# Layer-0 attentions: the keys are spread over the heads by ScalarE from the accumulator

## The chip, the cores and the metric

The kernel runs on one core of one Trainium2 chip, in fp32 throughout. The metric is the device time of one execution in microseconds. Before the change the median of three runs is 1980.87 us (1977.02 to 1982.0).

## The reference, cut to what matters

A two-layer perceiver block over 64 sequences of 32 queries with 256 features, 16 heads of 16 features, and a context of 257 rows. Each layer is a cross-attention, a self-attention and an FFN, each with a layernorm ahead and a residual. What the change touches are the two attentions of layer 0:

```python
# cross-attention X0: causal mask over the first 32 context rows
q = (layernorm(x) @ Wq.T + bq); k = (ctx @ Wk.T + bk); v = (ctx @ Wv.T + bv)     # 16 heads of 16
sm = softmax(where(causal, -inf, q k^T / sqrt(16)))
x = x + (sm v) @ Wo.T + bo
# self-attention A0: as above, with a bias by distance and a sigmoid gate
q, k, v = split(layernorm(x) @ Wqkv + bqkv)
out = softmax(q k^T / 4 + pos_bias, causal) v
x = x + (out * sigmoid(layernorm(x) @ Wgate + bgate)) @ Wout + bout
```

## The kernel before, in words

The 64 sequences of 32 rows lie in 16 tiles of 128 rows (4 sequences each, `SPT`). Both attentions of layer 0 run over the 16 tiles as 4 rounds of 4 lanes (`run_lanes`, `SLOTS0` = 20 slots). A tile's work is cut into steps with a slot each; lane `l` runs 5 slots behind lane `l-1`. Every engine walks the same slots and issues its steps in that fixed order; the engines meet through semaphores. Per stretch of five slots each engine handles one tile's worth of work, made up of steps of four different lanes.

Per tile, in the order of slots: VectorE takes statistics (slot 0) and normalizes (1, `d_scale`); TensorE turns the tile (2, `p_turn`, L408) and ScalarE copies it (3, L787); TensorE projects queries, keys and values, and in A0 the gate (4, `p_project`, L396), into the lane's two PSUM banks, transposed: features on partitions, rows on columns. ScalarE then evacuates (5, `a_keys`, `a_values`, `a_gate`): two instructions for the keys into `kT` (L796, with bias), two for the queries (L799, scale 0.25 and bias), two for the values (L807), in A0 two more for the gate (L825). VectorE (6, `d_keys`, L1020) multiplies `kT` into `kbd`: every key block of 32 columns is written four times, each copy multiplied with one of the four columns of `mask_hr`, which keeps the features of one head in each half of the partitions; so one matmul on `kbd` gives the scores of four heads. Behind it VectorE transposes the values (6, L1026), which GpSimd spreads (7, L1444). TensorE makes the scores (8, `p_scores`, L474) when `k_masked`, `qT_copied` and `v_copied` are there. VectorE adds the mask (9, L1052), takes the negative maximum (L1061) and subtracts (L1065); ScalarE takes the exponential (10, L831); VectorE sums (11, L1070); TensorE turns the probabilities (11, L483), ScalarE copies them (12, L835), TensorE multiplies with the values (13, L493), VectorE normalizes (14, L1089), TensorE turns (15, L502), ScalarE copies in X0 (16, L813) or VectorE multiplies with the gate in A0 (16, L1097), TensorE projects out (17, `p_out`, L402), VectorE adds to x (18, L1102).

So, where several lanes meet, ScalarE's order in one stretch of five slots is: exponential of one lane, then keys, queries, values (and gate) of another, then the copy L813 of a third (X0), the copy L835 of the first, the copy L787. VectorE's order is: statistics, in A0 L1097, sums, `d_keys`, value transpose, normalization, in A0 the gate's reciprocal (L1083) and addition (L1078), in A0 between them pieces of the quantization of FFN weights, L1102, L1089, mask, maximum, subtraction. TensorE's is: turn of the output, turn of the probabilities, output projection, turn, values, scores, projection.

Of the kernel before, what the change touches and what calls it, by code (L numbers as in the profile page):

```python
# [11 lines left out]
ALU = mybir.AluOpType  # L12
ACT = mybir.ActivationFunctionType
AX = mybir.AxisListType

P = 128
D = 256
KI = D // P
NSEQ = 64
L = 32  # L20
S = 257
T = NSEQ * L // P
SPT = P // L
H = 16
HD = D // H
G = 4
J = H // G
# [16 lines left out]
def perceiver(nc, A, out):  # L44
    ctx = ExitStack()
    with ctx:
        def sb(name, shape, dt=F32):
            return ctx.enter_context(nc.sbuf_tensor(name, shape, dt))

        def sem(name):  # L50
            return ctx.enter_context(nc.semaphore(name))
# [8 lines left out]
        mask_hr = sb("mask_hr", [P, 4])  # L60
        mask4 = sb("mask4", [P, 4])
# [7 lines left out]
        colb = sb("colb", [P, 10, KI])  # L69
        BQ0, BK0, BV0, BQA, BKA, BVA, BG, BQ1, BK1, BV1 = range(10)  # L70
        a1_bv = sb("a1_bv", [P, KI])
        nbg = sb("nbg", [P, KI])
        qb = sb("qb", [P, 2, KI])
        rowb = sb("rowb", [P, 4, D])
        BO0, BOA, BO1, BOB = range(4)
        a1_bqk = sb("a1_bqk", [P, 2 * D])
# [14 lines left out]
        def view(at, *shape):  # L91
            size = 1
            for s in shape:
                size *= s
            assert at + size <= RSIZE
            v = R[:, at:at + size]
            if len(shape) == 2:
                v = v.rearrange("p (a b) -> p a b", b=shape[1])
            elif len(shape) == 3:
                v = v.rearrange("p (a b c) -> p a b c", b=shape[1], c=shape[2])  # L100
            elif len(shape) == 4:
                v = v.rearrange("p (a b c d) -> p a b c d", b=shape[1], c=shape[2], d=shape[3])
            return v

        def put(at, sizes):
            places = []
            for s in sizes:
                places.append(at)
                at += s
            return places  # L110


        lane_at = [put(l * LANE, [256, 256, 2048, 512, 1024, 512, 256, 256, 256, 512]) for l in range(NL)]
# [4 lines left out]
        vq = [view(a[1], D) for a in lane_at]  # L118
        kbd = [view(a[2], 2048) for a in lane_at]
        om = [view(a[2], D) for a in lane_at]  # L120
        kT = [view(a[3], D) for a in lane_at]
        qT1 = [view(a[3], 512) for a in lane_at]
        pT = [view(a[3], G, P) for a in lane_at]
        vbd = [view(a[4], H, J * HD) for a in lane_at]
# [24 lines left out]
        a = put(W0, [512] * 4 + [1536, 512, 512])  # L149
# [29 lines left out]
        a = put(0, [256, 256, 512] + [KI * S] * 6 + [512] * 4 + [G * S] * 2 + [1024, 64, 256, 128, 128])  # L179
# [16 lines left out]
        a = put(R1, [KI * F1, KI * F1, NF1 * F1])  # L196
        f_w1, f_w2 = view(a[0], KI, F1), view(a[1], KI, F1)
        f_h1 = view(a[2], NF1, F1)
        a = put(0, [1024, 1024, 4096, 4096, 1024, 512, NF1 * F1, NF1 * D])
# [21 lines left out]
        posmask_ready, gate_bias_ready, pl_scale_ready, consts_made = map(  # L221
            sem, ("posmask_ready", "gate_bias_ready", "pl_scale_ready", "consts_made"))
# [3 lines left out]
                 "probs_ready sum_ready pT_ready pT_copied o_ready o_normed oT_ready oT_copied oT_gated "  # L226
                 "gate_exp gate_plus gate_done y_ready x_updated "
                 "lines_in lines_mul lines_step lines_sq lines_sum q_slots k_slots "
                 "qk_slots_ready q_evac kT_copied").split()
        s = {n: sem(n) for n in names}  # L230


        def tile(n, l):

            return NL * n + l + 1
# [52 lines left out]
        X0, A0, A1 = "x0", "a0", "a1"  # L288
# [3 lines left out]
        def run_lanes(eng, slots, stages):  # L292


            lag = slots // NL

            def a_round(i, steps, i_behind, steps_behind):
                for slot in range(slots):
                    for l in sorted(range(NL), key=lambda l: -((slot - lag * l) % slots)):

                        of_round, n = (steps_behind, i_behind) if slot < lag * l else (steps, i)
                        for at, step in of_round:
                            if at == (slot - lag * l) % slots:
                                step(l, n)

            behind = ()
            for enter, steps in stages:
                enter()
                a_round(0, steps, NT - 1, behind)
                with eng.Fori(1, NT) as i:  # L310
                    a_round(i, steps, i - 1, steps)
                behind = steps
            a_round(NT, (), NT - 1, behind)

        BASE = {X0: 0, A0: NT, A1: 2 * NT}
# [5 lines left out]
        BIAS_K = {X0: BK0, A0: BKA}  # L321
# [3 lines left out]
        bank = [[ps[:, 2 * l + i, :] for i in range(2)] for l in range(NL)]  # L325
# [454 lines left out]
        def _(act):  # L780
            for m in free["act"]:
                act.sem_inc(m, 1)
            af = nc.scalar.activation
# [5 lines left out]
            def a_keys(kind, l, n):  # L789
                if kind == A1:  # L790
                    act.wait_ge(s["qk_slots_ready"], tile(n - BASE[A1], l))
                    af(qT1[l], bank[l][0], ACT.Copy).then_inc(s["qT_copied"], 1)
                    return
                act.wait_ge(s["qk_ready"], tile(n, l))
                for fo in range(KI):
                    af(kT[l][:, fo * P:(fo + 1) * P], bank[l][0][:, (KI + fo) * P:(KI + fo + 1) * P],  # L796
                       ACT.Identity, bias=colb[:, BIAS_K[kind], fo:fo + 1]).then_inc(s["kT_copied"], 1)
                for fo in range(KI):
                    r = af(qT[l][:, fo * P:(fo + 1) * P], bank[l][0][:, fo * P:(fo + 1) * P],  # L799
                           ACT.Identity, scale=0.25, bias=qb[:, BIAS_Q[kind] // BQA, fo:fo + 1])  # L800
                r.then_inc(s["qT_copied"], 1)
# [33 lines left out]
                af(pT[l], bank[l][1].rearrange("p (g t) -> p g t", t=P), ACT.Copy).then_inc(s["pT_copied"], 1)  # L835

            act.wait_ge(in_const, 16 * N_CONST)
            act.wait_ge(gate_bias_ready, 3)
            act.wait_ge(consts_made, 1)

            def attention(kind, steps):
# [9 lines left out]
            for m in range(3):  # L851
                for c in range(3):
                    act.wait_ge(wT_turned, 3 * m + c + 1)
                    at = WT + 1536 * m + 512 * c
                    af(view(at, 512), ps[:, (3 * m + c) % 8, :], ACT.Copy).then_inc(wT_copied, 1)
            ugb = ug.rearrange("p f (b t) -> p f b t", t=BLK)
            with act.Fori(0, NB // 2) as i:
                for u in range(2):
                    b = 2 * i + u
# [10 lines left out]
            for f in range(NF0):  # L870
                af(ug[:, f + NF0, :], ug[:, f + NF0, :], ACT.Identity, scale=qinv[:, QG:QG + 1],
                   bias=magic[:, :]).then_inc(f0_gr, 1)
# [15 lines left out]
            with act.Fori(0, NF0) as f:  # L888
                af(ug[:, f + NF0, :], ug[:, f + NF0, :], ACT.Identity, scale=qinv[:, QS:QS + 1],
                   bias=magic[:, :]).then_inc(f0_g2r, 1)  # L890
            act.wait_ge(f0_scale, 4)
            with act.Fori(0, NB // 2) as i:
                for u in range(2):
                    b = 2 * i + u
# [3 lines left out]
                    for f in range(NF0):  # L898
                        af(oq[u][:, f, :], ugb[:, f, b, :], ACT.Identity, scale=qinv[:, QO:QO + 1],
                           bias=magic[:, :]).then_inc(f0_or, 1)  # L900
# [4 lines left out]
            for fo in range(KI):  # L905
                r = af(c_vlast[:, fo, :], ps[:, 2, fo * NSEQ:(fo + 1) * NSEQ], ACT.Identity,
                       bias=colb[:, BV1, fo:fo + 1])
# [80 lines left out]
        def _(dve):  # L988
            for m in free["dve"]:
                dve.sem_inc(m, 1)  # L990
            v = nc.vector
# [15 lines left out]

            def d_keys(kind, l, i, n):

                if kind == A1:  # L1010
                    dve.wait_ge(s["qk_slots_ready"], tile(n - BASE[A1], l))
                    k = bank[l][1].rearrange("p (c k) -> p c k", k=L).unsqueeze(2).broadcast_to([P, H, J, L])
                    m = mask4[:, :].unsqueeze(1).unsqueeze(3).broadcast_to([P, H, J, L])
                    v.tensor_tensor(kbd[l].rearrange("p (c j k) -> p c j k", j=J, k=L), k, m, ALU.mult)\
                        .then_inc(s["k_masked"], 1)
                    return
                dve.wait_ge(s["kT_copied"], KI * tile(n, l))
                k = kT[l].rearrange("p (c k) -> p c k", k=L).unsqueeze(2).broadcast_to([P, 8, 4, L])
                m = mask_hr[:, :].unsqueeze(1).unsqueeze(3).broadcast_to([P, 8, 4, L])
                v.tensor_tensor(kbd[l][:, 0:8 * P].rearrange("p (c h k) -> p c h k", h=4, k=L), k, m, ALU.mult)\  # L1020
                    .then_inc(s["k_masked"], 1)

            def d_turn_values(kind, l, i, n):
# [128 lines left out]
            def attention(kind, steps, enter=lambda: None):  # L1152
                return (enter, [(at, lambda l, i, step=step: step(
                    kind, l, i, i + (NORM if step in (d_norm, d_scale) else BASE)[kind])) for at, step in steps])
# [5 lines left out]
            v.tensor_scalar(nbg[:, :], colb[:, BG, :], -1.0, None, ALU.mult).then_inc(gate_bias_ready, 1)  # L1160
            for n, at in enumerate((BQ0, BQA)):
                v.tensor_scalar(qb[:, n, :], colb[:, at, :], 0.25, None, ALU.mult).then_inc(gate_bias_ready, 1)
            dve.wait_ge(in_x, 32)

            def enter_a0():
# [8 lines left out]
                dve.wait_ge(in_w["nat"], 48)  # L1174

            run_lanes(dve, SLOTS0, [
                attention(X0, [(0, d_norm), (1, d_scale), (6, d_keys), (6, d_turn_values), (9, d_mask), (9, d_max),
                               (9, d_shift), (11, d_sums), (14, d_norm_out), (18, d_add)]),
                attention(A0, [(0, d_norm), (1, d_scale), (6, d_keys), (6, d_turn_values), (7, d_gate1), (9, d_mask),
                               (9, d_max), (9, d_shift), (11, d_sums), (12, d_gate2), (14, d_norm_out),  # L1180
                               (16, d_gate_out), (18, d_add),
                               (2, d_w_max), (3, d_w_scale), (4, d_w_inverse), (8, d_w_divide), (12, d_w_round),
# [20 lines left out]
            for t in range(T):  # L1203
                r = v.tensor_scalar(xall[:, t, :], x[:, t, :], f_mv[:, t, 0:1], f_rstd[:, t:t + 1],
                                    ALU.subtract, ALU.mult)
# [5 lines left out]
            with dve.Fori(0, NB // 2) as i:  # L1211
                for u in range(2):
                    b = 2 * i + u
# [41 lines left out]
            with dve.Fori(0, NB // 2) as i:  # L1255
                for u in range(2):
                    b = 2 * i + u
# [10 lines left out]
            for par2 in range(2):  # L1268
                r = v.tensor_copy(c_kT[par2][:, :, S - 1], colb[:, BK1, :])
# [91 lines left out]
            for l in range(NL):  # L1361
                v.memset(qs[l], 0.0)
                r = v.memset(ks[l], 0.0)
# [277 lines left out]
```

## Time and profile before

| | |
|---|---|
| median of three runs | 1980.87 us |
| the profiled execution | 1977.1 us |
| its span | 1975.1 us |
| TensorE busy | 1587.7 us (80%) |
| VectorE busy | 871.9 us (44%) |
| ScalarE busy | 568.4 us (29%) |
| GpSimd busy | 522.9 us (26%) |
| mean granted clock of TensorE | 0.906 |
| X0 | about 21 to 140 us |
| A0 | about 140 to 305 us |

The profile is that of one execution. Shares of the whole span say little here, since the stages have different limits: the layer-1 cross-attention and FFN make up most of the span. What matters for X0 and A0 is read within their stretches: busy time by stretch, the instructions in order of time, and the chain of waits that ended last. An engine name in brackets at the end of a timeline row is what released the instruction after the idle time given.

### The profile page before, as it was taken

The page shows a single profiled execution, that of the slowest core. Times are in us where ns is not written, and L with a number is a line of the kernel's source. Part 1 is how long each engine was busy: PE and PEld are TensorE (multiplying, and loading weights), DVE is VectorE, ACT ScalarE, POOL GpSimd, SP SyncE. Part 2 cuts the span into 40 slices and gives each one's busy share as a digit, 9 for nine tenths or more (in the row PEclk, how much of TensorE's full clock was granted, in tenths as well). Part 3 has the DMA queues.
Part 4 walks back from the last instruction along what each step waited for, and adds up shares of the span by engine and source line. Part 5 has one row for each costly group of instructions (what it writes and reads, how often), then busy time and mean ns, then how long its engine had stood idle before and what let it go on. Part 6 is the DMA issues. An engine that isn't in the chain of part 4 may idle for free.

```text
span 1975.1 us, 31007 instructions
## 1 busy us (share of the span) xinstructions
PE 1587.7 (80%) x11788; PEld 1013.7 (51%) x11788; DVE 871.9 (44%) x1668; ACT 568.4 (29%) x1401; POOL 522.9 (26%) x587
## 2 busy tenths in 40 slices
PE   4887775890078999999994566667999999999999
PEld 3676653340067677777772444443445445445445
DVE  3889997337823565555554555553101101100100
ACT  2443332338323445444441111112111111111100
POOL 2443331006103444444443555551000000000000
PEclk9999997995589999999995777778999999999999
DMA  6000000000004111111100000002000000000000
GB/s 234 20 6 2 1 0 1 0 0 0 0 0 178 40 41 37 37 38 42 37 22 1 1 1 0 0 0 107 0 0 11 0 0 11 0 0 11 0 0 11
DMA packets 17765, 43.96 MB, mean 22 GB/s; under 512 B 2992, under 2 KB 5552, under 8 KB 16944
## 3 DMA queue, kind: packets, MB, share of 16 engines
q1 hardware_dynamic: 17712, 43.24, 6.6%
q8 instruction: 35, 0.57, 0.1%
q14 instruction: 18, 0.15, 0.0%
HBM read 41.14 MB, written 2.10 MB: 22 GB/s over the span
## 4 chain that ended last, share of the span: by engine, by line
PE 63%; DVE 16%; issue 9%; POOL 6%; ACT 4%; DVEq 1%; DMA 1%; SPq 0%; POOLq 0%; ACTq 0%
PE ps L754 22%; PE ps L396 12%; PE ps L603 6%; PE ps L609 6%; PE ps L629 4%; PE ps L402 3%; PE ps L769 3%; PE ps L573 3%; POOL lrn L1534 2%; PE ps L640 2%; DVE R L1005 2%; DVE R L1083 1%; POOL R L1524 1%; DVE nmx L1061 1%; DVE R L1233 1%
## 5 line engine op out<-in xcount | busy, mean ns | idle before, releaser
L754 PE MATMUL ps<-R 128*128 128x512 f32 x1024 | 440.6, 592 | 0.0
L396 PE MATMUL ps<-R 128*128 128x128 f32 (+1 forms) x1344 | 317.0, 396 | 7.7 <-ACT R L864 3.3
L754 PEld LDWEIGHTS ps<-R 128*128 128x128 f32 x1024 | 194.3, 190 | 243.5 <-issue 243.5
L396 PEld LDWEIGHTS ps<-R 128*128 128x128 f32 x1344 | 195.3, 199 | 126.7 <-issue 122.5
L1400 DVE TENSOR_TENSOR R<-ps,w3s 128x256 f32<-128x256 f32 x16 | 6.8, 425 | 465.1 <-PE ps L769 465.1
L1494 POOL TENSOR_TENSOR R<-R,c_inv 128x1024 f32<-128x1024 f32 x64 | 122.3, 1911 | 228.6 <-DVE c_inv L1338 228.6
L1303 DVE COPY R<-ps 128x512 f32<-128x512 f32 x128 | 88.5, 692 | 127.7 <-PE ps L629 127.7
L927 ACT ACTIVATE R<-ps,c_nmx 128x257 f32<-128x257 f32 x256 | 118.0, 474 | 89.7 <-DVE c_nmx L1327 89.7
L573 PE MATMUL ps<-R 128*128 128x256 f32 x192 | 50.0, 428 | 109.7 <-DVE R L1196 109.7
L609 PE MATMUL ps<-x_wv,R 128*128 128x256 f32 x512 | 131.2, 380 | 0.0
L603 PE MATMUL ps<-R,x_wk 128*128 128x256 f32 x512 | 125.2, 387 | 3.9 <-POOL R L1486 1.6
L1444 POOL TENSOR_TENSOR R<-R,mask 128x1024 f32<-128x1024 f32 x48 | 93.2, 1941 | 61.6 <-DVE R L1026 61.6
L603 PEld LDWEIGHTS ps<-R,x_wk 128*128 128x128 f32 x512 | 94.2, 192 | 23.1 <-issue 9.2
L573 PEld LDWEIGHTS ps<-R 128*128 128x128 f32 x192 | 41.6, 219 | 118.5 <-issue 104.9
L1555 POOL TENSOR_SCALAR g_ve<-g_mv 128x4 f32<-128x4 f32 x4 | 0.9, 231 | 355.7 <-DVE g_mv L1382 355.7
L609 PEld LDWEIGHTS ps<-x_wv,R 128*128 128x128 f32 x512 | 87.8, 191 | 7.0
L629 PE MATMUL ps<-ident,R 128*128 128x128 f32 x512 | 82.3, 284 | 5.0 <-DVE R L1303 2.6
L1486 POOL TENSOR_TENSOR R<-R 128x512 f32<-128x512 f32 x64 | 66.5, 1039 | 73.2 <-DMA R<-in_ctxT 73.2
L1327 DVE TENSOR_REDUCE c_nmx<-ps 128x2 f32<-128x514 f32 x128 | 82.3, 684 | 4.1 <-PE ps L619 4.0
L408 PE MATMUL ps<-ident,R 128*128 128x128 f32 x96 | 25.2, 353 | 70.2 <-DVE R L1005 70.2
L979 ACT ACTIVATE R<-ps,ffn_s 128x512 f32<-128x512 f32 x32 | 22.0, 687 | 197.5 <-PE ps L754 197.5
L831 ACT ACTIVATE R<-R 128x512 f32<-128x512 f32 x48 | 30.2, 630 | 168.7 <-DVE R L1065 168.7
(174 smaller groups left out, 2373.8 us busy)
## 6 DMA issues: line engine op xcount, KB each, us to landing
R<-in_ctxT SPq DMA_DIRECT2D x64, 257.0 KB, 2.7
R<-in_f_h SPq DMA_DIRECT2D x2, 4096.0 KB, 15.6
R<-in_f_w SPq DMA_DIRECT2D x3, 1024.0 KB, 8.4
R<-in_ctxk SPq DMA_DIRECT2D x16, 128.0 KB, 2.2
out<-x SPq DMA_DIRECT2D x4, 512.0 KB, 2.6
x<-in_x SPq DMA_DIRECT2D x1, 1792.0 KB, 9.2
R<-in_a_wqkv SPq DMA_DIRECT2D x1, 768.0 KB, 8.7
R<-in_w_up SPq DMA_DIRECT2D x1, 768.0 KB, 9.7
```

What stands on the lines that cost most here:

```text
L396: r = mm(dst, w[:, ki, fo * P:(fo + 1) * P], src[:, ki, :], start=(ki == 0), stop=(ki == KI - 1))
L573: r = mm(ps[:, 4 * u + t, 0:D], oq[u][:, f, t * P:(t + 1) * P], wdT[:, f, :], start=(f == 0), stop=(f == NF0 - 1))
L603: r = mm(ps[:, 4, fo * D:(fo + 1) * D], x1_wk[:, ki, fo * P:(fo + 1) * P], c_ctx[u][:, ki, 0:2 * P], start=(ki == 0), stop=(ki == KI - 1))
L609: r = mm(ps[:, 5, c * D:(c + 1) * D], c_ctx[u][:, ki, c * P:(c + 1) * P], x1_wv[:, ki, :], start=(ki == 0), stop=(ki == KI - 1))
L629: r = tr(ps[:, 6, at:at + P], c_p[par][:, g, c * P:(c + 1) * P], ident[:])
L754: r = mm(ps[:, ring[o % 4], :], w[:, k, o * P:(o + 1) * P], src[:, k, :], start=(k == 0), stop=(k == NF1 - 1))
L927: af(c_p[par][:, g, :], ps[:, g, 0:S], ACT.Exp, bias=c_nmx[par][:, g:g + 1], accum_out=c_sum[par][:, g:g + 1]).then_inc(c_exp, 1)
L1303: v.tensor_copy(c_pT[:, 2 * k:2 * k + 2, :, :].rearrange("p g c t -> p (g c t)"), ps[:, 6, :])\
L1327: v.tensor_reduce(c_nmx[u % 2][:, 2 * half:2 * half + 2], ps[:, 2 * half:2 * half + 2, 0:S], AX.X, ALU.max, negate=True).then_inc(c_max, 1)
L1444: p.tensor_tensor(vbd[l].rearrange("p c (r e) -> p c r e", e=HD), vq[l].rearrange("p (c e) -> p c e", e=HD).unsqueeze(2).broadcast_to([P, ...
L1486: p.tensor_tensor(c_ctx[u][:, :, 0:S - 1], c_ctx[u][:, :, 0:S - 1], c_ctx[u][:, :, S - 1:S].broadcast_to([P, KI, S - 1]), ALU.subtract).th ...
L1494: p.tensor_tensor(c_p[u % 2][:, :, 0:S - 1], c_p[u % 2][:, :, 0:S - 1], c_inv[u % 2][:, :].unsqueeze(2).broadcast_to([P, G, S - 1]), ALU.m ...
```

## The change

`a_keys` of X0 and A0 no longer writes `kT`. For each of the two halves of the features, ScalarE reads the projected keys in PSUM four times, once for each head column `h`, and writes them to their places in `kbd` (blocks of 32 columns, 128 apart) with the per-partition scale `mask_hr[:, h]` and a per-partition bias `kb`, which is the key bias times the same mask. The last of the eight instructions signals `k_masked`. VectorE's `d_keys` stays for the attention of layer 1 only; the buffer `kT` and its semaphore go. `kb` is made by two small VectorE operations at the start, and ScalarE waits for five instead of three signals of that kind before it begins. Queries, values and all else keep their code and order.

```diff
--- before.py
+++ after.py
@@ -71,6 +71,7 @@
         a1_bv = sb("a1_bv", [P, KI])
         nbg = sb("nbg", [P, KI])
         qb = sb("qb", [P, 2, KI])
+        kb = sb("kb", [P, 2, KI, 4])
         rowb = sb("rowb", [P, 4, D])
         BO0, BOA, BO1, BOB = range(4)
         a1_bqk = sb("a1_bqk", [P, 2 * D])
@@ -118,7 +119,6 @@
         vq = [view(a[1], D) for a in lane_at]
         kbd = [view(a[2], 2048) for a in lane_at]
         om = [view(a[2], D) for a in lane_at]
-        kT = [view(a[3], D) for a in lane_at]
         qT1 = [view(a[3], 512) for a in lane_at]
         pT = [view(a[3], G, P) for a in lane_at]
         vbd = [view(a[4], H, J * HD) for a in lane_at]
@@ -226,7 +226,7 @@
                  "probs_ready sum_ready pT_ready pT_copied o_ready o_normed oT_ready oT_copied oT_gated "
                  "gate_exp gate_plus gate_done y_ready x_updated "
                  "lines_in lines_mul lines_step lines_sq lines_sum q_slots k_slots "
-                 "qk_slots_ready q_evac kT_copied").split()
+                 "qk_slots_ready q_evac").split()
         s = {n: sem(n) for n in names}
 
 
@@ -793,8 +793,12 @@
                     return
                 act.wait_ge(s["qk_ready"], tile(n, l))
                 for fo in range(KI):
-                    af(kT[l][:, fo * P:(fo + 1) * P], bank[l][0][:, (KI + fo) * P:(KI + fo + 1) * P],
-                       ACT.Identity, bias=colb[:, BIAS_K[kind], fo:fo + 1]).then_inc(s["kT_copied"], 1)
+                    k = bank[l][0][:, (KI + fo) * P:(KI + fo + 1) * P].rearrange("p (b k) -> p b k", k=L)
+                    spread = kbd[l][:, fo * SPT * P:(fo + 1) * SPT * P].rearrange("p (b h k) -> p h b k", h=4, k=L)
+                    for h in range(4):
+                        r = af(spread[:, h], k, ACT.Identity, scale=mask_hr[:, h:h + 1],
+                               bias=kb[:, BIAS_K[kind] // BQA, fo, h:h + 1])
+                r.then_inc(s["k_masked"], 1)
                 for fo in range(KI):
                     r = af(qT[l][:, fo * P:(fo + 1) * P], bank[l][0][:, fo * P:(fo + 1) * P],
                            ACT.Identity, scale=0.25, bias=qb[:, BIAS_Q[kind] // BQA, fo:fo + 1])
@@ -835,7 +839,7 @@
                 af(pT[l], bank[l][1].rearrange("p (g t) -> p g t", t=P), ACT.Copy).then_inc(s["pT_copied"], 1)
 
             act.wait_ge(in_const, 16 * N_CONST)
-            act.wait_ge(gate_bias_ready, 3)
+            act.wait_ge(gate_bias_ready, 5)
             act.wait_ge(consts_made, 1)
 
             def attention(kind, steps):
@@ -1007,17 +1011,10 @@
 
             def d_keys(kind, l, i, n):
 
-                if kind == A1:
-                    dve.wait_ge(s["qk_slots_ready"], tile(n - BASE[A1], l))
-                    k = bank[l][1].rearrange("p (c k) -> p c k", k=L).unsqueeze(2).broadcast_to([P, H, J, L])
-                    m = mask4[:, :].unsqueeze(1).unsqueeze(3).broadcast_to([P, H, J, L])
-                    v.tensor_tensor(kbd[l].rearrange("p (c j k) -> p c j k", j=J, k=L), k, m, ALU.mult)\
-                        .then_inc(s["k_masked"], 1)
-                    return
-                dve.wait_ge(s["kT_copied"], KI * tile(n, l))
-                k = kT[l].rearrange("p (c k) -> p c k", k=L).unsqueeze(2).broadcast_to([P, 8, 4, L])
-                m = mask_hr[:, :].unsqueeze(1).unsqueeze(3).broadcast_to([P, 8, 4, L])
-                v.tensor_tensor(kbd[l][:, 0:8 * P].rearrange("p (c h k) -> p c h k", h=4, k=L), k, m, ALU.mult)\
+                dve.wait_ge(s["qk_slots_ready"], tile(n - BASE[A1], l))
+                k = bank[l][1].rearrange("p (c k) -> p c k", k=L).unsqueeze(2).broadcast_to([P, H, J, L])
+                m = mask4[:, :].unsqueeze(1).unsqueeze(3).broadcast_to([P, H, J, L])
+                v.tensor_tensor(kbd[l].rearrange("p (c j k) -> p c j k", j=J, k=L), k, m, ALU.mult)\
                     .then_inc(s["k_masked"], 1)
 
             def d_turn_values(kind, l, i, n):
@@ -1160,6 +1157,9 @@
             v.tensor_scalar(nbg[:, :], colb[:, BG, :], -1.0, None, ALU.mult).then_inc(gate_bias_ready, 1)
             for n, at in enumerate((BQ0, BQA)):
                 v.tensor_scalar(qb[:, n, :], colb[:, at, :], 0.25, None, ALU.mult).then_inc(gate_bias_ready, 1)
+            for n, at in enumerate((BK0, BKA)):
+                v.tensor_tensor(kb[:, n, :, :], colb[:, at, :].unsqueeze(2).broadcast_to([P, KI, 4]),
+                                mask_hr[:, :].unsqueeze(1).broadcast_to([P, KI, 4]), ALU.mult).then_inc(gate_bias_ready, 1)
             dve.wait_ge(in_x, 32)
 
             def enter_a0():
@@ -1174,9 +1174,9 @@
                 dve.wait_ge(in_w["nat"], 48)
 
             run_lanes(dve, SLOTS0, [
-                attention(X0, [(0, d_norm), (1, d_scale), (6, d_keys), (6, d_turn_values), (9, d_mask), (9, d_max),
+                attention(X0, [(0, d_norm), (1, d_scale), (6, d_turn_values), (9, d_mask), (9, d_max),
                                (9, d_shift), (11, d_sums), (14, d_norm_out), (18, d_add)]),
-                attention(A0, [(0, d_norm), (1, d_scale), (6, d_keys), (6, d_turn_values), (7, d_gate1), (9, d_mask),
+                attention(A0, [(0, d_norm), (1, d_scale), (6, d_turn_values), (7, d_gate1), (9, d_mask),
                                (9, d_max), (9, d_shift), (11, d_sums), (12, d_gate2), (14, d_norm_out),
                                (16, d_gate_out), (18, d_add),
                                (2, d_w_max), (3, d_w_scale), (4, d_w_inverse), (8, d_w_divide), (12, d_w_round),
```

## Rows read from the trace of the kernel before

**Rows 1.** Stretches in X0, A0: us, busy us by engine (instructions), clock, DMA share, GB/s
```profile
21.00:137.00 116.00, 95.02 (x1473) 79.06 (x1474) 89.88 (x176) 50.00 (x148) 52.40 (x61) 1.00 0.16 57
149.00:305.00 156.00, 115.65 (x1625) 94.92 (x1624) 150.51 (x302) 54.69 (x171) 52.66 (x59) 0.96 0.00 1
```

**Rows 2.** Chain of waits within X0, 90 to 106 us: start, us, what
```profile
92.37 0.70 DVE R L1065
93.10 0.63 ACT R L831
...
94.63 0.64 ACT R L807 x2
...
97.54 0.68 PE ps L474 x32
...
99.69 0.70 DVE R L1065
```

**Rows 3.** Timeline of X0, same tile: start, us, engine, line, operation, [idle before <-releaser]
```profile
94.65 1.16 DVE L1020 TENSOR_TENSOR R<-R,mask_hr 128x1024 f32<-128x1024 f32 x1
...
95.60 1.13 PE L402 MATMUL ps<-R 128*128 128x256 f32 x4 [1.16 <-ACT R L813]
95.73 0.43 DVE L1026 STREAM_TRANSPOSE R<-R 128x256 f32<-128x256 f32 x1
```

**Rows 4.** Timeline of A0, ninth of its sixteen tiles and the last
```profile
227.44 0.69 DVE L1065 TENSOR_TENSOR R<-R,nmx 128x512 f32<-128x512 f32 x1
...
228.16 0.63 ACT L831 ACTIVATE R<-R 128x512 f32<-128x512 f32 x1 [5.57 <-DVE R L1065]
...
229.69 0.64 ACT L807 ACTIVATE R<-ps,colb 128x128 f32<-128x128 f32 x2
...
230.49 1.16 DVE L1020 TENSOR_TENSOR R<-R,mask_hr 128x1024 f32<-128x1024 f32 x1
...
231.57 0.43 DVE L1026 STREAM_TRANSPOSE R<-R 128x256 f32<-128x256 f32 x1
...
301.47 0.69 DVE L1065 TENSOR_TENSOR R<-R,nmx 128x512 f32<-128x512 f32 x1
...
304.84 0.43 DVE L1026 STREAM_TRANSPOSE R<-R 128x256 f32<-128x256 f32 x1
```

**Rows 5.** ScalarE: single instructions, then groups by form (busy us, mean ns)
```profile
93.63 0.35 ACT L796 ACTIVATE R<-ps,colb 128x128 f32<-128x128 f32 x1
93.88 0.36 ACT L796 ACTIVATE R<-ps,colb 128x128 f32<-128x128 f32 x1
...
L871 ACT ACTIVATE R<-R,magic,qinv 128x2048 f32<-128x2048 f32 x6 | 12.0, 2082 | 2.0 <-DVE qinv L1191 2.0
...
L883 ACT ACTIVATE R<-R,magic 128x2048 f32<-128x2048 f32 x6 | 11.6, 1985 | 0.0
```

**Rows 6.** TensorE in A0, timeline; then stretches: us, busy, clock, DMA share, GB/s
```profile
221.74 0.44 PE L408 MATMUL ps<-ident,R 128*128 128x128 f32 x2 [1.48 <-DVE R L1005]
...
222.69 0.67 PE L474 MATMUL ps<-R 64*32 64x128 f32 x32
...
232.35 0.69 PE L408 MATMUL ps<-ident,R 128*128 128x128 f32 x2 [1.30 <-DVE R L1005]
...
233.98 1.11 PE L474 MATMUL ps<-R 64*32 64x128 f32 x32
...
230.00:240.00 10.00, 8.70 (x104) 0.66 0.00 0
...
1263.00:1264.00 1.00, 0.00 (x0) 1.00 0.00 0
...
1265.00:1266.00 1.00, 0.69 (x2) 0.50 0.00 0
```

**Rows 7.** VectorE at the start, timeline
```profile
18.30 0.43 DVE L998 BATCH_NORM_STATS2 stats<-x 128x6 f32<-128x256 f32 x1 [8.11 <-DMA x<-in_x]
...
28.15 1.23 DVE L1020 TENSOR_TENSOR R<-R,mask_hr 128x1024 f32<-128x1024 f32 x1 [6.45 <-ACT R L796]
```

## The prediction

> **What bounds the kernel now.** The change touches only the two attentions of layer 0, X0 (cross-attention, from about 21 to 140 us) and A0 (self-attention, to about 305 us), sixteen tiles each. I read the busy time by stretch first [rows 1]. VectorE is busy for 89.88 of 116 us in X0 and for 150.51 of 156 us in A0, ScalarE for 50.00 and 54.69. By shares alone one would take VectorE for the bound of both stages and ScalarE for an engine with half its time to give away. In X0 a quarter of VectorE is idle all the same, so I followed the chain of waits there for one tile [rows 2]. It closes on itself: subtraction of the maximum on VectorE (92.37), exponential on ScalarE (93.10), the evacuations of keys, queries and values of another lane (keys from the exponential's start plus 0.53, values at 94.63), the evacuation of the turned output, the output projection on TensorE (95.60 [rows 3]), turn, values and scores (scores from 97.54), then mask, maximum and subtraction again (99.69). From subtraction to subtraction it is 7.32 us, and ScalarE's key evacuations are a link of it. The VectorE multiply that the change removes is not: it begins at 94.65, and the transpose that follows at 95.73, while TensorE waits 1.16 us for ScalarE [rows 3]. So X0 is bound by a ring through three engines, and ScalarE's order of work stands in it.
>
> In A0 VectorE has little idle time, and its own order is the bound: subtraction at 227.44, the multiply at 230.49, the value transpose at 231.57 [rows 4]. ScalarE runs beside it: exponential at 228.16, values at 229.69. From subtraction to transpose it is 4.13 us in this tile, 3.37 us in the last one [rows 4], and read the same way over all sixteen tiles 3.36 to 4.99, 4.03 us on average (64.5 in all).
>
> **The price of one new evacuation.** Two key evacuations of 128x128 become eight of the same size, each with a per-partition scale and a per-partition bias in place of a bias alone. The old kind is issued every 0.25 us: the first starts at 93.63, the second at 93.88 [rows 5]. For 2048 columns, the form with two such operands takes 2082 ns, the one with a bias alone 1985 ns [rows 5], so the second operand costs 97 ns. I carry this over to 128 columns, where no row has both: 0.25 + 0.095 = about 0.345 us from one start to the next. Bounds: 0.25 us if the second operand is hidden in a short instruction. Downwards, 1985 ns for 2048 columns is 0.97 ns a column with the fixed cost spread over them, 0.12 us for 128 columns; that is the value if next to all fixed cost were hidden, and I use it as the floor. Upwards, its whole duration without overlap, 0.36 + 0.10 = 0.46 us. I take 0.345, as the same addition is seen at the same type of instruction; that the output now lies in four runs of 32 I cost at nothing. Eight cost 2.76 us instead of 0.50, +2.26 us a tile.
>
> The Trainium skill, page "ScalarE: Activation LUTs", section "What ACT_TABLE_LOAD costs", says that each per-partition pointer operand adds about 93 ns to an activation; the 97 ns here agree. Its sum, 186 + 2 x 93 + 107 ns less an overlap of 93, would be an estimate of 0.37 us an instruction, thus some 0.2 us more a tile than mine. The same page's rules for kernel authors say to multiply and add on VectorE rather than on ScalarE, which speaks against this change.
>
> **X0.** The eight evacuations lie in the ring, before those of queries and values, and nothing else is late there: every tile takes 2.26 us more, 9.58 instead of 7.32. The multiply's 1.08 us on VectorE gives nothing back, as it ran beside ScalarE. The transpose, formerly behind the multiply, now waits for the values alone and comes about 0.7 us after their start; the normalization behind it ends about 0.7 us later still, while TensorE is in the output projection (1.13 us), so it makes nobody late. The first tile has TensorE's projection as its releaser and pays about 1.5 us, as there VectorE waits for the keys and its multiply of 1.23 us did lie on the path, partly beside the values [rows 7]; the last has about 1 us of VectorE's entry work into A0 as cover. 1.5 + 15 x 2.26 - 1 = about +34 us.
>
> **A0.** Removed from VectorE: 231.57 - 230.49 = 1.08 us a tile. But the transpose also waits for ScalarE's values. From the subtraction: 0.72 to the exponential, 0.53 of it, 2.76 for the keys, 0.50 for the queries, then the values, whose end lets the transpose start 0.65 later: 5.16 us. So the new gap is 5.16 us against 4.03 on average; VectorE is relieved and then stands waiting. 16 x 5.16 = 82.5, less 64.5, is +18 us. The other half of the period, from the transpose to the next subtraction, is VectorE's own work and stays. Behind the waiting transpose stand the normalization of another lane, the reciprocal and everything else; GpSimd's spreading of the values waits for the transpose but has several steps in hand. The gate's evacuation comes 0.5 us after the values and is needed only after the reciprocal.
>
> **TensorE's clock.** In X0 it is granted in full (1.00, 2.4 GHz) and in A0 0.96 [rows 1]. It falls to the lower level (0.50, 1.2 GHz) where TensorE has paused: in the layer-1 attention nothing runs at 1263 to 1264 and the clock is 0.50 at 1265 to 1266. In A0, where the pauses ahead of the turn are 1.3 to 1.5 us, some stretches already have a fall, as that with 0.66, and most have none [rows 6]. The new ring makes one unbroken pause of about 1.2 + 2.26 = 3.4 us a tile in X0. I expect falls in most X0 tiles. The price: from turn to the end of the scores it is 235.09 - 232.35 = 2.74 us at the low level and 223.36 - 221.74 = 1.62 at the high one [rows 6], +1.1 us on the ring. In A0 this part is hidden behind VectorE. Bounds: nothing, and sixteen tiles of 1.9 us with a slower output projection too, 30 us. I take 12 tiles x 1.1 = +13 us, an assumption as to the number.
>
> **The rest.** Two more small VectorE operations build the masked biases, and ScalarE waits for five of them; VectorE waits 8.11 us for x at that point anyway [rows 7], so this costs nothing, and some 0.5 us if it had no cover. No DMA changes. Nothing after A0 changes.
>
> **Sum.** 34 + 18 + 13 = +65 us. Against the profiled execution (1977.1 us, with a span of 1975.1) that gives 2042; the median of the runs is 1980.87, 3.8 above it, so I predict 2046 us.
>
> **Rivals.** (a) The clock stays high, all else as above: +52, 2033 us. For it speaks that it stays at 1.00 through all of X0 with TensorE busy 82%; against it, the pause of 3.4 us. (b) The second operand is hidden, 0.25 us an instruction: 1.5 us a tile in X0, +23; in A0 the gap is 4.4 us, +6; with a few clock falls +5: 2015 us. Against it: the pointer's price is plain at 2048 columns. (c) Faster: the fixed cost is hidden wherever evacuations stand in a row, so that each costs 0.12 us. From 0.20 us an instruction down, A0's gap is shorter than now. At 0.12 it is 3.4 us, a gain of 0.6 x 16 = 10 us, against 0.46 x 16 = 7 lost in X0: 1978 us; if VectorE were the bound in both stages and ScalarE never late, 32 x 1.08 = 35 us would be saved, 1946. Both are against the 0.25 us seen now and against the ring. (d) Each evacuation takes the full 0.46 us, or the clock falls everywhere: 8 x 0.115 = 0.9 us a tile more over 32 tiles, +29, or +17 for the clock: 2063 to 2075 us. That the change does not do what it says I exclude: the multiply is gone, and its product is formed by the scale.
>
> **How the numbers follow.** My forecast 0.5, (a) 0.2, (b) 0.13, (c) 0.03, (d) 0.12, no difference 0.02. A measurement of this kernel can tell about 0.3% (6 us) from no change. All cases but (c) and the last are slower by more: faster 0.03, same 0.03, slower 0.94. The range takes in (a), (b) nearly, and the lower half of (d): 2013 to 2068.
>
> **What would show it.** In X0 the distance from subtraction to subtraction grows to about 9.6 us, or 10.7 at a low clock, eight starts of about 0.34 us stand between exponential and queries, and the transpose waits for the value evacuation in both stages. In A0 VectorE's busy time falls by 17 us, while the wait of the transpose for ScalarE is new and the period grows to about 11.4 us. Wrong would be: starts 0.25 us apart (b), a transpose that does not wait (c), a clock of 1.00 in X0 (a), or a stage after 305 us that takes another time.

## The result, and the profile after

| | before | after |
|---|---|---|
| median | 1980.32 us | 2048.19 us |
| profiled execution | 1977.1 us | 2049.11 us |
| its span | 1975.1 us | 2047.3 us |
| VectorE busy | 871.9 us | 840.2 us |
| ScalarE busy | 568.4 us | 641.4 us |

The medians are those of four runs each; the fourth of the kernel before moves its median from 1980.87 to 1980.32. The ratio is 1.035, with an interval of 1.0326 to 1.0374. VectorE does 32 us less, ScalarE 73 us more, and the kernel is 68 us slower. The last value transpose of X0 starts at 192.19 where it started at 140.68, the last one of A0 at 376.67 where it started at 304.84. So X0 lost 51.5 us and A0 20.3; the span as a whole is 72.2 us longer, which leaves less than half a microsecond for everything behind.

Two stretches, inside X0 and inside A0 (us, then busy us of TensorE, its weight loads, VectorE, ScalarE and GpSimd with counts, TensorE's clock, DMA share, GB/s), to be read against [rows 1]:

```profile
21.00:175.00 154.00, 107.22 (x1354) 88.96 (x1353) 66.81 (x144) 78.66 (x222) 48.17 (x56) 0.82 0.12 42
188.00:375.00 187.00, 138.45 (x1747) 114.48 (x1745) 144.10 (x307) 96.17 (x281) 56.49 (x64) 0.86 0.00 1
```

VectorE is idle for more than half of X0 now, and for nearly a quarter of A0; TensorE's clock is down from 1.00 to 0.82 and from 0.96 to 0.86. One tile of X0 in the timeline of the changed kernel (start, us, engine, line, operation, idle time before it and what ended it), to be read against [rows 2, 3]:

```profile
99.95 0.63 ACT L835 ACTIVATE R<-R 128x512 f32<-128x512 f32 x1 [3.91 <-DVE R L1062]
...
100.48 2.88 ACT L799 ACTIVATE R<-ps,kb,mask_hr 128x128 f32<-128x128 f32 x8
...
103.22 0.66 ACT L803 ACTIVATE R<-ps,qb 128x128 f32<-128x128 f32 x2
103.72 0.68 ACT L811 ACTIVATE R<-ps,colb 128x128 f32<-128x128 f32 x2
...
104.43 0.45 DVE L1023 STREAM_TRANSPOSE R<-R 128x256 f32<-128x256 f32 x1 [2.84 <-ACT R L811]
...
104.72 2.07 PE L402 MATMUL ps<-R 128*128 128x256 f32 x4 [3.39 <-ACT R L817]
...
107.15 1.08 PE L493 MATMUL ps<-R 128*32 128x64 f32 x32
...
110.39 0.69 DVE L1062 TENSOR_TENSOR R<-R,nmx 128x512 f32<-128x512 f32 x1
111.00 0.42 DVE L1002 BATCH_NORM_STATS2 stats<-x 128x6 f32 x1
111.11 0.63 ACT L835 ACTIVATE R<-R 128x512 f32<-128x512 f32 x1 [3.47 <-DVE R L1062]
```

The eight evacuations take 103.22 - 100.48 = 2.74 us, 0.3425 each. The transpose has waited 2.84 us for ScalarE, TensorE's output projection 3.39. And that projection takes 2.07 us, where it took 1.13. The reason stands in the clock (us, busy, clock, DMA share, GB/s):

```profile
102.00:103.00 1.00, 0.00 (x0) 1.00 0.38 117
103.00:104.00 1.00, 0.00 (x0) 1.00 0.00 0
104.00:105.00 1.00, 0.28 (x1) 0.86 0.00 0
105.00:106.00 1.00, 1.00 (x3) 0.50 0.00 0
```

After a pause of 3.39 us the clock falls to 0.50 just as TensorE begins. By an arm of the ring I mean one of the two branches of waits that meet again in TensorE's turn: ScalarE's leads over the evacuations and the output projection to it, VectorE's over the value transpose and the normalization. In A0 the same evacuations of ScalarE decide the start of VectorE's transpose, to be read against [rows 4]:

```profile
278.77 0.69 DVE L1062 TENSOR_TENSOR R<-R,nmx 128x512 f32<-128x512 f32 x1
...
280.04 2.88 ACT L799 ACTIVATE R<-ps,kb,mask_hr 128x128 f32<-128x128 f32 x8
...
283.27 0.68 ACT L811 ACTIVATE R<-ps,colb 128x128 f32<-128x128 f32 x2
...
283.98 0.45 DVE L1023 STREAM_TRANSPOSE R<-R 128x256 f32<-128x256 f32 x1 [1.85 <-ACT R L811]
```

From subtraction to transpose it is 5.21 us, and 5.20 to 5.22 in each of the sixteen tiles, where it was 3.36 to 4.99.

### The profile page after: what moved, and what is told of

Read it like the earlier page. It is cut to its first block, busy times and chain, and to the rows that moved or that the text cites. A ratio compares the mean times of both kernels' runs of the same rounds, so it can differ in the third digit from the quotient of the medians.

```text
span 2047.3 us, 31151 instructions
## 1 busy us (share of the span) xinstructions
PE 1627.5 (79%) x11788; PEld 1046.9 (51%) x11788; DVE 840.2 (41%) x1638; ACT 641.4 (31%) x1593; POOL 522.6 (26%) x587
## 4 chain that ended last, share of the span: by engine, by line
PE 62%; DVE 13%; ACT 9%; issue 8%; POOL 6%; DMA 1%; DVEq 0%; SPq 0%; POOLq 0%; ACTq 0%
PE ps L754 21%; PE ps L396 12%; PE ps L603 6%; PE ps L609 5%; ACT R L799 4%; PE ps L629 3%; PE ps L402 3%; PE ps L769 3%; PE ps L573 2%; POOL lrn L1534 2%; PE ps L640 2%; DVE R L1009 2%; POOL R L1524 1%; DVE R L1062 1%; DVE nmx L1058 1%
## 5 line engine op out<-in xcount | busy, mean ns | idle before, releaser
L396 PE MATMUL ps<-R 128*128 128x128 f32 (+1 forms) x1344 | 331.7, 411 | 7.7 <-ACT R L868 3.3
L754 PEld LDWEIGHTS ps<-R 128*128 128x128 f32 x1024 | 194.3, 190 | 243.5 <-issue 243.5
L396 PEld LDWEIGHTS ps<-R 128*128 128x128 f32 x1344 | 209.6, 213 | 130.0 <-issue 126.0
L573 PE MATMUL ps<-R 128*128 128x256 f32 x192 | 48.5, 418 | 109.4 <-DVE R L1196 109.4
L573 PEld LDWEIGHTS ps<-R 128*128 128x128 f32 x192 | 40.4, 213 | 117.8 <-issue 104.6
L799 ACT ACTIVATE R<-ps,kb,mask_hr 128x128 f32<-128x128 f32 x256 | 92.3, 465 | 5.1 <-PE ps L396 5.1
L402 PE MATMUL ps<-R 128*128 128x256 f32 x128 | 45.4, 487 | 52.5 <-ACT R L817 49.2
```

Source lines behind the costliest of these rows:

```text
L396: r = mm(dst, w[:, ki, fo * P:(fo + 1) * P], src[:, ki, :], start=(ki == 0), stop=(ki == KI - 1))
L402: r = mm(dst, src[:, ki, :], w[:, ki], start=(ki == 0), stop=(ki == KI - 1))
L573: r = mm(ps[:, 4 * u + t, 0:D], oq[u][:, f, t * P:(t + 1) * P], wdT[:, f, :], start=(f == 0), stop=(f == NF0 - 1))
L754: r = mm(ps[:, ring[o % 4], :], w[:, k, o * P:(o + 1) * P], src[:, k, :], start=(k == 0), stop=(k == NF1 - 1))
L799: r = af(spread[:, h], k, ACT.Identity, scale=mask_hr[:, h:h + 1], bias=kb[:, BIAS_K[kind] // BQA, fo, h:h + 1])
```

## The experiments

The theory is that of the prediction: a ring through ScalarE in X0, ScalarE's arm ahead of the transpose in A0, 0.34 us an instruction because of the second operand, and TensorE's clock on top in X0. The rivals: ScalarE's load costs the same in every tile; the write in short runs and not the operand makes the instruction long; TensorE's part of the ring is longer for another reason than its pause.

In the cuts of code below, `...` and words in brackets stand for code that is left out, and comments are mine.

### The change in one stage only

In `e1_x0_only` the eight evacuations serve X0 and the old path A0:

```diff
+                if kind == X0:      # e2_a0_only: A0
+                    (the eight evacuations, k_masked)
+                else:
                     for fo in range(KI):
                         af(kT[l][:, fo * P:(fo + 1) * P], ...
-                attention(X0, [(0, d_norm), (1, d_scale), (6, d_keys), (6, d_turn_values), ...
+                attention(X0, [(0, d_norm), (1, d_scale), (6, d_turn_values), ...
```

> ScalarE spreads the keys in X0 only; A0 keeps the two evacuations and VectorE's multiply. Ring theory: X0 alone takes its whole loss, +51 us over the kernel before (2032 us), of it 35 us by the eight evacuations and 16 by TensorE's clock. Rival (the load of ScalarE as such costs, equally per tile in both stages): +36 us, 2016.

Measured: 2031.05 us, 1.026 of the kernel before (1.0228 to 1.0293), some 51 us, with an interval from 45 to 58. That 51 us were expected is no forecast of its own, as the trace of the changed kernel already had 51.5 in X0; the prediction had 34 + 13 = 47. In its trace the sixteen gaps of A0 from subtraction to transpose add up to 64.4 us, as in the kernel before (64.5).

> ScalarE spreads the keys in A0 only; X0 as before. Ring theory: the gap from subtraction to value transpose goes from 4.03 us on average to 5.2 in A0, +20 us over the kernel before (2000 us); together with the X0-only kernel the two losses add up to the whole, 72 us. Rival (equal loss per tile): +36 us, 2016; the naive reading of VectorE as A0's bound: -17 us.

Measured: 1991.88 us, ratio 1.0075 (1.0046 to 1.0104), some 15 us, with an interval from 9 to 21. The sixteen gaps are 5.2 us each, 83.5 in all, 19.0 more than before. The two losses add up to the whole within their intervals, and they are far from equal: ScalarE's load does not cost the same in every tile; what it costs depends on where in the stage it is late.

### The fall of the clock

`e3_fill` gives TensorE something to do in the pause, without any effect on the result: the turn of the probabilities, whose evacuation is not due yet, is made five times.

```diff
-                for g in range(G):
-                    r = tr(bank[l][1][:, g * P:(g + 1) * P], pr[l][:, J * g:J * (g + 1), :], ident[:])
+                for again in range(5 if kind == X0 else 1):
+                    for g in range(G):
+                        r = tr(bank[l][1][:, g * P:(g + 1) * P], pr[l][:, J * g:J * (g + 1), :], ident[:])
                 r.then_inc(s["pT_ready"], 1)
```

> The changed kernel with TensorE's pause in X0 filled: the turn of the probabilities is made five times over, with the same data to the same place, which is some 2.2 us more of work for TensorE where it waits for ScalarE. If the falls of the clock in X0 cost what lies beyond 2.24 us a tile, the clock there goes from 0.82 to about 1.00, the period in X0 from 10.8 to about 9.6 us, and the time falls by about 17 us, to 2031. Rival (TensorE's part of the ring grew for another reason, such as the transpose coming late): more work on TensorE changes nothing or adds up to 2 us a tile: 2048 to 2080.

Measured: 2028.75 us, ratio 1.0263 (1.0233 to 1.0292), so about 17 us less than the changed kernel by their ratios, with more work done: the turns take 2.41 us instead of 0.60, 1.8 us more. Its timeline in X0, and its stretch from 21 to 190 us (columns as in the stretches above):

```profile
112.56 2.41 PE L484 MATMUL ps<-ident,R 128*128 128x128 f32 x20
116.67 1.13 PE L402 MATMUL ps<-R 128*128 128x256 f32 x4 [1.70 <-ACT R L818]
...
21.00:190.00 169.00, 137.02 (x1945) 121.15 (x1945) 88.87 (x192) 96.07 (x273) 58.65 (x69) 0.99 0.11 39
```

The pause is 1.70 us instead of 3.4, the clock stays at 0.99, and the projection takes 1.13 us again. The transposes of X0 follow each other at 9.60 us, from the fourth tile to the last; the last of them is at 173.97 instead of 192.19, 18.2 us earlier. That is the price of the clock in X0, and the rest, 9.60 - 7.32 = 2.28 us a tile, is that of the evacuations.

### The price of the second operand

`e4_one_operand` leaves the bias of the keys out; it adds the same to all scores of a row, which the softmax takes away again.

```diff
-                        r = af(spread[:, h], k, ACT.Identity, scale=mask_hr[:, h:h + 1],
-                               bias=kb[:, BIAS_K[kind] // BQA, fo, h:h + 1])
+                        r = af(spread[:, h], k, ACT.Identity, scale=mask_hr[:, h:h + 1])
```

> The changed kernel without the bias of the keys in layer 0 (it adds the same to all scores of a row, so the softmax doesn't see it): the eight evacuations have one per-partition operand, the scale. If the second operand costs 0.093 us each, starts are 0.25 us apart instead of 0.343, the gap from subtraction to transpose falls from 5.21 to 4.46 us in both stages, and the time by 16 x 0.74 in X0 and 16 x 0.7 in A0, with a few falls of the clock less: 2048 - 24 to 28, about 2022. Rival (the interval is that of a write in four runs of 32 columns, not of the operand): 0.343 stays, 2048 stays.

Measured: 2019.93 us, ratio 1.0223 (1.0191 to 1.0254), about 25 us less than the changed kernel by the ratios. ScalarE and then TensorE in X0:

```profile
112.52 2.16 ACT L799 ACTIVATE R<-ps,mask_hr 128x128 f32<-128x128 f32 x8
114.52 0.68 ACT L802 ACTIVATE R<-ps,qb 128x128 f32<-128x128 f32 x2
...
116.04 2.07 PE L402 MATMUL ps<-R 128*128 128x256 f32 x4 [2.72 <-ACT R L816]
```

Eight in 2.00 us, 0.25 each, with the same writes in four runs of 32 columns: the operand is the cause, at 0.0925 us apiece, and the runs cost nothing. The gap from subtraction to transpose is 4.49 us. The clock has not come back in X0: this kernel's period is 10.24 to 10.29 us there from the seventh tile on, against 8.82 by the evacuations alone (7.32 + 8 x 0.25 - 0.50; in two early tiles 8.87 is seen), although its pause is 0.7 us shorter: the output projection still takes 2.07 us. So in this ring shortening the pause from 3.4 to about 2.7 us is not enough, and filling it to 1.7 us is. This run is also the prediction's rival (b) made real: it would have had +34 us, and the ratio gives +44. A0's gaps grow by 7.3 us where (b) had 6; the rest of the difference is the clock, which (b) had at 5 us in all and which alone makes 1.42 us of each period of 10.24.

### What comes next in the ring

`e5_order` moves ScalarE's keys, queries and values of X0 one slot later, so that the copy for the output projection goes ahead of them.

```diff
-                attention(X0, [(3, a_xnT), (5, a_keys), (5, a_values), (10, a_exp), (12, a_pT), (16, a_oT)]),
+                attention(X0, [(3, a_xnT), (6, a_keys), (6, a_values), (10, a_exp), (12, a_pT), (16, a_oT)]),
```

> The changed kernel with ScalarE's keys, queries and values of X0 one slot later, behind the copy of another lane's turned output. The output projection is then no longer behind the eight evacuations, and it cuts TensorE's pause in two. At a full clock the turn comes as late as before by the other arm of the ring (values, transpose, normalization: 5.7 us after the exponential either way), so the gain is what the falls of the clock cost, up to 0.9 us a tile or more: 2030 to 2040 against 2048. Theory that ScalarE's load alone sets the period: no difference, 2048.

Measured: 2062.14 us, ratio 1.043 (1.041 to 1.0449): slower than the changed kernel, against my expectation. Its timeline in X0 tells why:

```profile
114.61 4.64 PE L396 MATMUL ps<-R 128*128 128x128 f32 x24
...
119.09 0.38 PE L502 MATMUL ps<-ident,R 128*128 128x128 f32 x2
...
119.51 0.38 ACT L817 ACTIVATE R<-ps 128x256 f32<-128x256 f32 x1 [1.92 <-PE ps L502]
119.79 2.90 ACT L799 ACTIVATE R<-ps,kb,mask_hr 128x128 f32<-128x128 f32 x8
...
124.55 0.44 PE L408 MATMUL ps<-ident,R 128*128 128x128 f32 x2 [3.47 <-DVE R L1009]
```

The copy at the head of ScalarE's row waits for TensorE's turn of the output, and that stands behind the projection of queries, keys and values (L396), which here, for the most part at the low clock, takes 4.64 us instead of 2.94. In every second tile it is about 3.7 us and the period 11.3 instead of 12.6. I had put the copy ahead without asking when its input is there: the whole projection is in the ring now, the eight evacuations start only when it is done, and the pause ahead of the turn is as long as ever. The theory that ScalarE's load sets the period falls too, as the load is the same.

### Without ScalarE's key evacuations

If ScalarE's evacuations are the ring, the other direction should pay: none at all. VectorE can multiply straight from the accumulator, since the key bias isn't needed. It waits for the queries' evacuation, so that the two engines read the bank one after the other.

```diff
-                for fo in range(KI):
-                    af(kT[l][:, fo * P:(fo + 1) * P], ...).then_inc(s["kT_copied"], 1)
...
-                dve.wait_ge(s["kT_copied"], KI * tile(n, l))
-                k = kT[l].rearrange("p (c k) -> p c k", k=L)...
+                dve.wait_ge(s["qT_copied"], tile(n, l))
+                k = bank[l][0][:, KI * P:2 * KI * P].rearrange("p (c k) -> p c k", k=L)...
...
-                attention(X0, [(0, d_norm), (1, d_scale), (6, d_keys), (6, d_turn_values), ...
+                attention(X0, [(0, d_norm), (1, d_scale), (6, d_turn_values), (7, d_keys), ...   # e6 only
```

> The kernel before without any key evacuation and without the key bias (the softmax doesn't see it): VectorE multiplies straight from the accumulator, after the queries' evacuation, and in X0 one slot later, behind the transpose and the normalization. Ring theory: two evacuations leave the ring of X0 and VectorE's arm gets shorter too, so X0's period is 6.82 instead of 7.32 us, -7.5 us; A0 stays, as VectorE is the bound there and its multiply costs the same from PSUM. 0.4% below the kernel before, about 1969 to 1973. Rival: the multiply is slower from PSUM (0.1 us or more each in A0): no difference.

> The same, with the multiply in its old place ahead of the transpose. Ring theory with two arms: ScalarE's arm gets 0.5 us shorter, but VectorE's (sums, multiply, transpose, normalization, turn) was only 0.04 us ahead of it, and takes over: X0's period stays at 7.27 to 7.32 us, no difference to the kernel before (within 0.1%). If ScalarE's arm alone were the ring: -7.5 us, as in the one above.

Measured: `e6_direct7` 1967.09 us, ratio 0.9953 (0.9938 to 0.9969), some 9 us less than the kernel before; `e7_direct6` 1974.19 us, ratio 0.9986 (0.9976 to 0.9996), some 3 us less where I had expected none within 0.1%. In X0, first of the one with the multiply behind the transpose, from one subtraction to the next:

```profile
87.63 0.69 DVE L1061 TENSOR_TENSOR R<-R,nmx 128x512 f32<-128x512 f32 x1
...
90.34 1.13 PE L401 MATMUL ps<-R 128*128 128x256 f32 x4 [0.65 <-ACT R L809]
...
90.70 1.22 DVE L1016 TENSOR_TENSOR R<-ps,mask_hr 128x1024 f32<-128x1024 f32 x1
...
94.43 0.69 DVE L1061 TENSOR_TENSOR R<-R,nmx 128x512 f32<-128x512 f32 x1
```

and then of the one with the multiply in its old place:

```profile
92.81 0.63 ACT L827 ACTIVATE R<-R 128x512 f32<-128x512 f32 x1 [3.04 <-DVE R L1061]
...
94.37 1.16 DVE L1016 TENSOR_TENSOR R<-ps,mask_hr 128x1024 f32<-128x1024 f32 x1
...
95.45 0.43 DVE L1022 STREAM_TRANSPOSE R<-R 128x256 f32<-128x256 f32 x1
95.80 0.37 DVE L1001 TENSOR_SCALAR R<-x,mv,rstd 128x256 f32 x1
...
96.23 0.44 PE L407 MATMUL ps<-ident,R 128*128 128x128 f32 x2 [0.30 <-DVE R L1001]
```

The first has a period of 6.80 us (6.82 expected). The second has 7.32 as before: the output projection is 0.5 us earlier, and TensorE then waits for the normalization, which stands behind multiply and transpose. The kernel before has two arms of nearly the same length in X0; cutting ScalarE's alone gives next to nothing, cutting both gives the 0.5 us. From the exponential to the turn it is 96.56 - 93.10 = 3.46 us in the kernel before, by ScalarE's arm, and 96.23 - 92.81 = 3.42 us in `e7_direct6`, by VectorE's. The turn in the kernel before:

```profile
96.56 0.39 PE L408 MATMUL ps<-ident,R 128*128 128x128 f32 x2
```

### The work shared in A0

`e8_shared` is `e6_direct7` with A0's keys shared: ScalarE spreads the first 128 features with four evacuations, VectorE multiplies the second 128.

```diff
+                if kind == A0:
+                    k = bank[l][0][:, KI * P:(KI + 1) * P].rearrange("p (b k) -> p b k", k=L)
+                    spread = kbd[l][:, 0:SPT * P].rearrange("p (b h k) -> p h b k", h=4, k=L)
+                    for h in range(4):
+                        af(spread[:, h], k, ACT.Identity, scale=mask_hr[:, h:h + 1])
...
+                c0 = 4 if kind == A0 else 0        # VectorE: blocks c0 to 8 of 8
```

> The kernel above with the later multiply, and in A0 the keys shared: ScalarE spreads the first half of the features (four evacuations with one operand, 1.0 us), VectorE multiplies the other half from the accumulator (512 columns, about 0.6 us). Ring theory: A0's gap from subtraction to transpose is the longer of ScalarE's 3.4 and VectorE's 3.6 us, against 4.03 now: -6 to -8 us in A0 besides -7.5 in X0: about 0.7% below the kernel before. Rival (no half measure helps, as one engine's gain is the other's loss): as the kernel above.

Measured: 1960.25 us, ratio 0.9915 (0.9899 to 0.9931), 17 us below the kernel before and, by the ratios, 86 below the changed one. One gap of A0, from subtraction to transpose:

```profile
216.39 0.69 DVE L1067 TENSOR_TENSOR R<-R,nmx 128x512 f32<-128x512 f32 x1
...
217.66 1.12 ACT L798 ACTIVATE R<-ps,mask_hr 128x128 f32<-128x128 f32 x4
...
219.16 0.66 ACT L808 ACTIVATE R<-ps,colb 128x128 f32<-128x128 f32 x2
...
219.44 0.63 DVE L1022 TENSOR_TENSOR R<-ps,mask_hr 128x512 f32<-128x512 f32 x1
219.99 0.43 DVE L1028 STREAM_TRANSPOSE R<-R 128x256 f32<-128x256 f32 x1
```

It is 3.60 us, the sixteen together 58.9 us against 64.5: -5.6 in A0, a little less than the 6 to 8 expected. Most of them stand at 3.54 to 3.63, as expected; the gain is smaller because of two of 3.8 and one of 4.71 us. In that one VectorE waits for TensorE's turn of the output, which comes behind a projection slowed by the low clock, 5.20 us instead of 3.84:

```profile
263.47 5.20 PE L395 MATMUL ps<-R 128*128 128x128 f32 x32
...
268.93 0.42 DVE L1099 TENSOR_TENSOR R<-ps,R 128x256 f32<-128x256 f32 x1 [1.49 <-PE ps L501]
```

## Why the prediction was right

- **The ring of X0** (step: the evacuations lie in it and nothing is late beside them): right. Without the fall of the clock the period is 9.60 us, as `e3_fill` shows, where I had 9.58. That VectorE's removed multiply gives nothing back there is seen in its idle time: it waits 2.84 us for the values. What I had not seen is how narrow the reading of the kernel before was: the multiply was no link of the ring by 0.04 us a tile at most, 3.46 against 3.42 us (`e7_direct6`). For the forecast this made no difference, as ScalarE's arm grew by 2.24 us.
- **The price of one evacuation**: 0.3425 us against 0.345, and `e4_one_operand` puts the difference on the second operand. The rival with 0.25 us is excluded, as is that of the runs of 32 columns. Sizing it by the pair of rows at 2048 columns [rows 5] carried over to 128 columns unchanged.
- **X0's end terms**: I had 1.5 us for the first tile; it was 30.49 - 29.85 = 0.6 us. This can't be told from chance: in `e2_a0_only`, with X0 as before, the same transpose starts at 28.66.
- **A0**: +18 us predicted. The gap was 5.21 us instead of 5.16 and the sixteen gaps grew by 18.8 us; the stage grew by 20.3. Of the rest 0.63 us lies between the last transpose of X0 and the next subtraction (5.45 instead of 4.82), and 0.78 behind the first transpose of A0 (6.46 instead of 5.68). That its second half would stay was right: from transpose to subtraction it is 5.97 to 6.79 us in the settled tiles of both kernels. From tile to tile A0 takes 11.59 us, where I had about 11.4.
- **The clock** was the one term that I assumed rather than read: 12 tiles at 1.1 us, +13. It was 18 us. The number of tiles was right and the price of one too low. Between the output projections at 60.44 and 182.03 there are twelve tiles, and in each the product with the values takes 1.04 to 1.08 us instead of 0.65. Their periods are 10.41 to 11.62 us, together 16.9 us above 9.60, or 1.4 a tile. The output projection belongs to it, which I had left to the bound: it takes 2.07 us instead of 1.13 in the five tiles where the fall comes ahead of it, 1.29 to 1.86 in three where it comes in the middle, and 1.13 in the four where it comes behind. From its start to the end of the scores it is 3.35 to 4.56 us instead of 2.54. The other 1.4 us of the 18 arose in the first two tiles and were not looked into. That so near a number of tiles came out was in part luck, since no row gave it.
- **The clock in A0** is lower too, 0.86, and was to cost nothing. In the sixteen gaps of the changed kernel it does cost nothing. But the 1.4 us at the border of the stages are for the most part its doing: there VectorE waits 0.58 us for the scores of one tile (196.20) and 0.46 for the product with the values of the next (207.28), and in `e3_fill`, with the clock at 0.99 in X0, the two distances are 4.38 and 5.66 us. And in the kernel before one of the sixteen gaps, that of 4.99 us, holds a wait of 1.24 us for TensorE's turn behind a projection of 4.96 us, where one at the high clock takes 3.84. So TensorE's part is hidden in A0 most of the time, not always.
- **The sum**: +65 us predicted, +68 by the medians and +72 by the profiled executions. The terms read off at 34, 18 and 13 us are 33, 20 and 18 by the traces. Right, and by its own mechanism; the missing part is the clock.
- **The Trainium skill's page** "ScalarE: Activation LUTs", section "What ACT_TABLE_LOAD costs", gives about 93 ns for a pointer operand: 0.0925 us here, measured by `e4_one_operand`. Its sum for the instruction, 186 + 2 x 93 + 107 - 93 = 386 ns, is 0.04 above the 0.3425 us seen here. I had put it at 0.37 us, wrongly added, and so 0.2 us a tile above mine where it would be 0.3; my sum did not rest on it.

What stays open: what decides whether the clock falls. The length of the pause ahead of the output projection alone does not. In X0 there was no fall after 1.70 us (`e3_fill`, in every tile), 1.98 and 2.22 us (`e4_one_operand`) and 2.62 us (the changed kernel), and there was one after 2.72 us and more. But in A0 of the changed kernel the clock stayed at 1.00 after a pause of 3.15 us (ending at 215.32), and in A0 of the kernel before it fell where no pause was longer than 1.5 us (the stretch with 0.66 in [rows 6]). No run separates the pause from how busy TensorE is around it; `e3_fill` changes both.

## What to carry to other kernels

An engine that is busy for 43% of a stage can still be on its critical ring: follow the chain of waits once around before work is moved to it, and move it only where it stands beside the ring. Count instructions before elements: eight evacuations of 128 columns cost 2.74 us where two cost 0.50, of it 0.09 us apiece for a second per-partition operand. And if a stage has two arms of nearly equal length, shorten both in one step, or none will show.

## What was not expected of the hardware

- TensorE with more to do made the kernel faster: with 1.8 us of superfluous turns in the pause, the clock in X0 was 0.99 instead of 0.82 and the execution about 17 us shorter.
- The price of a wait on TensorE is not the wait alone: the pause of 3.4 us had the work behind it, from output projection to scores, take 4.1 us (104.72 to 108.84) instead of 2.5 (95.60 to 98.14).
- VectorE's multiply of 1024 columns takes 1189 ns with the keys from PSUM in `e6_direct7` and 1169 ns from SBUF before (means of 32 each; 1171 ns from PSUM in `e7_direct6`), so reading straight from the accumulator is nearly free.
